# Turning the attention weighting around: context keys stationary, scaling after a trip through DRAM

## Chip, cores and metric

The kernel runs on one core of one Trainium2 chip. The metric is device time in microseconds (us) of one launch; lower is better.

## What is computed

For each of 32 batches of 128 tokens of width 128, the block adds a gated cross attention and then a gated mixture of experts:

```python
x = x + tanh(g_xattn) * attention(layernorm(x), ctx)      # 16 heads of 64; ctx: 128 keys of width 64
x = x + tanh(g_ffn)   * experts(layernorm(x))             # 32 experts, 8 picked per token of 2 of 4 groups, 1 shared
# attention: scores = (ln Wq)(ctx Wk)^T / 8; out = softmax(scores) (ctx Wv) Wo + bo
```

## The kernel before

The host only lays arrays out. Weights are folded once: Wq and Wk of a head become one 128 x 64 matrix (`a_hi`, `a_lo`), Wv and Wo one 64 x 128 matrix (`c_pair`, tanh of the gate in it). So a head is scores = (ln x A) ctx^T, u = exp(scores - max) ctx, output = (u / row sum) C. Two heads make a pair (q = 0, 1: rows 0 to 63 and 64 to 127), a batch has eight pairs, in two halves h of four pairs.

The 32 batches go in eight chunks of four (c, b; batch t = 4c + b). All synchronisation is written by hand with semaphores, and each engine runs its own list in program order: a wait holds everything behind it on that engine. The attention of one batch:

- TensorE, half 0: `max_scores` of batch t + 2 (tokens on partitions, for the row maxima), `scores` of t (keys on partitions), `transpose_max` of t + 1, `transpose_u` and two `weigh` of batch t - 1 (h = 1), `project_out` of t - 2. Half 1: `max_scores`, `scores`, `transpose_u` of t - 1, `weigh` of t (h = 0, q = 0 and 1). At odd b, `g_project` for half of the next chunk stands between those two `weigh`; at b = 1, `transpose_norm` (L1033) of the next chunk in half 0.
- `weigh` (L1097) has the probabilities as stationary matrix and the 64 context columns and a column of ones as moving one: four products of 65 columns for one (h, q). u stands with tokens on partitions, the row sum in its own column.
- VectorE: `take_max` (L706), two per half, `normalise` (L714, a reciprocal of four sums and a product that reads PSUM), `residual`, `g_low`, and the layer norm chains `ln_level` (L627): 14 levels of tiny instructions per chunk of four batches, once for the first norm (next chunk) and once for the second (previous chunk).
- ScalarE: `exp_of`, `max_out`, `ut_out` (u transposed, PSUM to SBUF), at odd b `g_high`. GpSimd splits contexts and expert weights into two halves and adds a bias. SyncE issues every DMA; `load_max_row` (L279) is the one in the loop that depends on fresh results.

Then the experts (`experts_of` on each engine): 17 units u per chunk, three engines deep; TensorE has nine products of 512 columns per unit, VectorE two, GpSimd one. Routing of chunk c + 1 (48 VectorE steps) and the second norm's application run between the units of chunk c. The routing weights go through DRAM (`store_rows`, then `load_group`, 2 x 256 KB broadcast) before `weigh_hidden` can use them. At the seam of attention and experts, the routing of chunk 0 runs beside the last attention chunk (`SEAM`).

## Time and profile before

| | |
|---|---|
| time, median of 3 runs | 703.14 us (701.32 to 707.08) |
| the profiled execution | 703.62 us, its span in the trace 701.8 us |
| TensorE busy (matmul) | 683.8 us, 97% |
| VectorE / ScalarE / GpSimd busy | 73% / 47% / 38% |
| granted TensorE clock, mean | 0.995 |

Spans are from first to last instruction; the 1.8 us between the span and its execution's time are outside every engine. Busy times come from one profiled execution. A busy TensorE only says that some matmul was in flight.

### The profile page before, as it was taken

How to read it: one execution, taken by the hardware profiler on the slowest of the kernel's cores; microseconds unless marked ns; L12 is line 12 of the kernel's file. 1: busy time of each engine (PE TensorE's matmuls, PEld its weight loads, DVE VectorE, ACT ScalarE, POOL GpSimd, SP SyncE). 2: the span in 40 equal slices, each digit the busy share in tenths (PEclk: the TensorE clock that was granted, in tenths of full speed). 3: DMA queues.
4: the chain of work that ended last, by engine and by line, in shares of the span. 5: the costliest groups of instructions: out<-in, count | busy, mean ns of one | idle time of the engine just before them, and what ended most of it. 6: DMA issues, size and time to landing. Idle time of an engine off the chain costs nothing.

```text
span 701.8 us, 15942 instructions
## 1 busy us (share of the span) xinstructions
PE 683.8 (97%) x4700; PEld 580.8 (83%) x4700; DVE 512.6 (73%) x1640; ACT 331.3 (47%) x627; POOL 266.2 (38%) x316
## 2 busy tenths in 40 slices
PE   8799999999999999999999898999999999999997
PEld 6589889888889889889998686878787888878785
DVE  6775877768767777687567596877778686969565
ACT  3243344434443344434344555555555555555553
POOL 4212121222122121212310264656666565756654
PEclk9999999999999999999999999999999999999999
DMA  5401000000000000000000554535363636455550
GB/s 134 131 19 27 17 19 18 22 18 18 18 18 18 19 17 18 24 18 18 18 2 1 115 131 95 136 90 138 86 160 79 165 91 155 106 124 136 111 148 15
DMA packets 44815, 47.27 MB, mean 67 GB/s; under 512 B 11744, under 2 KB 27232, under 8 KB 44768
## 3 DMA queue, kind: packets, MB, share of 16 engines
q1 hardware_dynamic: 44768, 46.72, 27.4%
q8 instruction: 21, 0.34, 0.2%
q14 instruction: 26, 0.21, 0.1%
HBM read 43.81 MB, written 2.62 MB: 66 GB/s over the span
## 4 chain that ended last, share of the span: by engine, by line
PE 89%; POOL 4%; issue 4%; DVE 1%; DMA 1%; ACT 0%; POOLq 0%; SPq 0%; DVEq 0%
PE bank L1105 16%; PE bank L1029 13%; PE bank L1031 13%; PE bank L1030 13%; PE bank L1137 8%; PE bank L1065 5%; PE bank L1113 5%; POOL halves L457 4%; PE bank L1085 3%; PE bank L1091 2%; PE bank L1088 2%; PE bank L1094 2%; PE bank L1152 1%; PE bank L1036 1%; PE bank L1075 1%
## 5 line engine op out<-in xcount | busy, mean ns | idle before, releaser
L457 POOL TENSOR_TENSOR halves<-area,halves 128x512 fp32r<-128x512 f32 x135 | 174.6, 1293 | 145.0 <-ACT halves L580 139.4
L537 ACT ACTIVATE area<-bank 128x512 f32<-128x512 f32 x128 | 69.5, 595 | 190.7 <-PE bank L1094 190.7
L593 ACT ACTIVATE area<-bank 128x512 f32<-128x512 f32 x136 | 81.3, 597 | 112.6 <-PE bank L1031 111.8
L989 DVE TENSOR_TENSOR bank<-area,bank 128x512 f32<-128x512 f32 x128 | 88.6, 692 | 55.4 <-PE bank L1031 54.7
L1105 PE MATMUL bank<-ctx_keys,area 128*128 128x65 f32 x1024 | 123.1, 271 | 0.0
L1105 PEld LDWEIGHTS bank<-ctx_keys,area 128*128 128x128 f32 x1024 | 120.6, 192 | 0.4 <-issue 0.4
L1029 PE MATMUL bank<-x2t_hi,w_hi 128*128 128x512 f32 x272 | 110.4, 406 | 2.2 <-DVE area L997 2.1
L1031 PE MATMUL bank<-x2t_lo,w_hi 128*128 128x512 f32 x272 | 107.0, 393 | 0.0
L710 DVE TENSOR_REDUCE row_max<-bank 128x4 f32<-128x512 f32 x128 | 82.0, 684 | 33.5 <-PE bank L1065 28.9
L1030 PE MATMUL bank<-x2t_hi,w_lo 128*128 128x512 f32 x272 | 106.5, 392 | 0.0
L405 POOL TENSOR_TENSOR ctx_hi<-ctx_raw,ones_col 128x128 fp32r<-128x128 f32 x32 | 12.8, 400 | 238.7 <-PE bank L1094 232.2
L580 ACT ACTIVATE halves<-area 128x512 fp32r<-128x512 f32 x136 | 85.0, 626 | 17.8 <-DVE area L997 12.8
L997 DVE TENSOR_TENSOR area<-bank,wbc 128x512 f32<-128x512 f32 x128 | 86.3, 679 | 3.6 <-DMA wbc<-rows_dram 3.6
L1137 PE MATMUL bank<-c_pair,area 128*128 128x128 f32 x512 | 63.8, 278 | 0.7 <-ACT area L490 0.7
L1029 PEld LDWEIGHTS bank<-x2t_hi,w_hi 128*128 128x128 f32 x272 | 51.4, 189 | 14.5 <-DVE area L997 4.3
L1031 PEld LDWEIGHTS bank<-x2t_lo,w_hi 128*128 128x128 f32 x272 | 51.3, 189 | 11.7
L723 DVE TENSOR_TENSOR area<-bank,inv_sum 128x256 f32<-128x256 f32 x128 | 54.3, 425 | 9.1
L1137 PEld LDWEIGHTS bank<-c_pair,area 128*128 128x128 f32 x512 | 59.7, 192 | 0.9 <-ACT area L490 0.9
L1030 PEld LDWEIGHTS bank<-x2t_hi,w_lo 128*128 128x128 f32 x272 | 51.6, 190 | 10.1
L1029 PE MATMUL bank<-halves,w_hi 128*128 128x512 f32 x136 | 54.3, 399 | 1.1 <-POOL halves L457 1.1
L1031 PE MATMUL bank<-halves,w_hi 128*128 128x512 f32 x136 | 53.9, 397 | 0.0
L1030 PE MATMUL bank<-halves,w_lo 128*128 128x512 f32 x136 | 53.9, 396 | 0.0
(119 smaller groups left out, 1099.0 us busy)
## 6 DMA issues: line engine op xcount, KB each, us to landing
wbc<-rows_dram SPq DMA_DIRECT2D x128, 256.0 KB, 4.4
w_raw<-experts SPq DMA_DIRECT2D x32, 102.0 KB, 2.0
ctx_raw<-ctx_t SPq DMA_DIRECT2D x64, 32.0 KB, 2.1
out<-area SPq DMA_DIRECT2D x7, 256.0 KB, 4.2
ctx_keys<-ctx_nat SPq DMA_DIRECT2D x32, 32.0 KB, 1.8
max_rows<-max_t SPq DMA_DIRECT2D x64, 4.0 KB
area<-wq_t SPq DMA_DIRECT2D x1, 512.0 KB, 4.6
area<-wo SPq DMA_DIRECT2D x1, 512.0 KB, 4.4
```

Source lines behind the costliest of these rows:

```text
L457: nc.gpsimd.tensor_tensor(hid_lo[:, u % SLOTS, :], hid[:, u % HIDS, :], raw(hid_hi[:, u % SLOTS, :]), ALU.subtract).then_inc(hidlo_ready, 1)
L537: nc.scalar.activation(probs_t[:, k, :, :], st_ps[q][:].rearrange("p (h n) -> p h n", h=4), ACT.Exp)\
L580: nc.scalar.activation(hid_hi[:, u % SLOTS, :], hid[:, u % HIDS, :], ACT.Copy).then_inc(hidhi_ready, 1)
L593: nc.scalar.activation(silu_g[:, u % 2, :], gate_ps[u % 2][:], ACT.Silu).then_inc(silu_ready, 1)
L710: nc.vector.tensor_reduce(row_max[:, parity, first:first + 4], ps[q][:].rearrange("p (h m) -> p h m", h=4), AX_X, ALU.max)\
L989: nc.vector.tensor_tensor(up_ps[u % UPS][:], silu_g[:, u % 2, :], up_ps[u % UPS][:], ALU.mult)\
L997: nc.vector.tensor_tensor(hid[:, u % HIDS, :], up_ps[u % UPS][:], wbc[:, group % WBC_SLOTS, i, :], ALU.mult).then_inc(hid_ready, 1)
L1029: nc.tensor.matmul(ps, wh, xh, start=start, stop=False)
L1030: nc.tensor.matmul(ps, wl, xh, start=False, stop=False)
L1031: return nc.tensor.matmul(ps, wh, xl, start=False, stop=stop)
L1105: ins = nc.tensor.matmul(u_ps[q][:, i * (CD + 1):(i + 1) * (CD + 1)], probs_t[:, k, i, :], ctx_keys[:, b, :], start=True, stop=True)
L1137: ins = nc.tensor.matmul(ps, u_t[:, parity, p, :], c_pair[:, p, :], start=p == 0, stop=p == PAIRS - 1)
```

## The change

- `weigh`: the context keys are the stationary matrix (65 columns: keys and ones for q = 0; 128 columns: ones, 63 zeros, keys for q = 1), the probabilities of four heads the moving one: one product of 512 columns per (h, q). u comes out transposed, with the row sums in partition 64 (q = 0) or 0 (q = 1). `transpose_u` and its evacuation `ut_out` go.
- ScalarE copies u from PSUM to SBUF (`u_out`, four per batch, 65 or 128 x 512) in place of two `ut_out`.
- Row sums: SyncE spreads each row of 1024 sums over 64 partitions (`spread_sums`, two DMAs), VectorE takes one reciprocal of 128 x 16 (`invert`), SyncE stores it to DRAM (`store_inverse`) and reads it back as a broadcast to 2 x 64 partitions (`spread_inverse`, two DMAs of 64 x 1024, one buffer). VectorE then scales u from SBUF with two instructions of 64 x 1024 (`normalise(t, ., q)`), both inputs in SBUF. The projection comes one batch later (t - 3 in place of t - 2).
- Layer norms: statistics are taken batch by batch (second norm) or all in the first chunk (first norm); the Newton chain runs over 4, 4 and 24 batches for the first norm and over 28 and 4 for the second.
- Seam: the second norm and the routing of chunk 0 start earlier, and the last batches' reciprocal, scaling, projection and residual (`LATE`, `NORM_AT`) move into the first experts' units; the last four batches' second norm moves into chunk 1. Routing of chunk 1 starts one unit earlier.
- `load_raw` is one DMA of 128 partitions, `load_keys` writes the keys twice.

```diff
-LN_STEPS = 2 * CB + 5 + 3 * NEWTON_STEPS
+RSTD_LEVELS = 3 + 3 * NEWTON_STEPS
+RSTD_STEPS = RSTD_LEVELS + 1
...
-LN_LEVELS = 5 + 3 * NEWTON_STEPS
-LN_AT = {0: range(0, 9), 1: range(9, 12), 2: range(12, LN_LEVELS)}
-LN2_AT = {4: range(0, 6), 5: range(6, 9), 6: range(9, LN_LEVELS)}
-SEAM = (1, 7, 11, 15, 18, 21)
+LN_AT = {0: range(0, 5), 1: range(5, 9), 2: range(9, RSTD_LEVELS)}
+AHEAD = 2
+STATS_AT = {3: (2,), 4: (3,), 5: (4,), 6: (5, 6), 7: (7,)}
+NB_SEAM = (NCH - 2) * CB
+SEAM = {4: (1, 7), 5: (7, 13), 6: (13, 16), 7: (16, 21)}
+LATE = {NB - 2: 5, NB - 1: 11}
+NORM_AT = {(2, 1): ((NB - 2, 0), (NB - 2, 1)), (6, 1): ((NB - 1, 0),), (7, 1): ((NB - 1, 1),)}
...
-        u_norm = area[:, 2:4, :].rearrange("p a (h q d) -> p a h q d", h=PAIRS, q=2)
+        u_even = area[:, 2:4, :].rearrange("p q (h n) -> p q h n", h=2)
...
-        ctx_keys = sb("ctx_keys", [P, CB, CD + 1])
+        ctx_keys = sb("ctx_keys", [P, CB, 3 * CD])
+        u_odd = sb("u_odd", [P, 2, 2, CT])
+        u_raw = (u_even, u_odd)
+        sums = sb("sums", [P, 2, HEADS])
+        inverse = sb("inverse", [P, 2, HEADS])
+        inverse_bc = sb("inverse_bc", [P, 2, CT])
...
+            def spread_sums(t, parity):
+                wait_first(u_ready, 4 * t + 4)
+                for q in range(2):
+                    row = CD if q == 0 else 0
+                    sp.dma_start(sums[rows(q), parity, :], u_raw[parity][row:row + 1, q, :, :]).then_inc(sums_in, 16)
+            def store_inverse(t, parity):
+                wait_first(inverse_ready, t + 1)
+                sp.dma_start(inverse_dram[parity].rearrange("q (p n) -> (q p) n", n=HEADS), inverse[:, parity, :])\
+                    .then_inc(inverse_out, 16)
+            def spread_inverse(t, parity):
+                wait_first(inverse_out, 16 * t + 16)
+                for q in range(2):
+                    wait_first(norm_ready[q], t)
+                for q in range(2):
+                    sp.dma_start(inverse_bc[rows(q), :, :].rearrange("p h n -> p (h n)"),
+                                 inverse_dram[parity, q:q + 1, :].broadcast_to([HD, 2 * CT])).then_inc(inverse_in, 16)
...
+                    if not (last and b == CB - 1):
+                        load_max_row(t + 1, (b + 1) % 2, t - 1)
+                    if not (first and b == 0):
+                        spread_sums(t - 1, (b - 1) % 2)
                     if not last:
                         wait_first(ctx_ready, t + 1)
                         load_raw(b, (t + CB) * P)
                     if not (last and b >= 2):
                         wait_first(wsplit_ready, t + 1)
                         load_weights(b % 2, (t + 2) * WSTEP)
-                    if not (last and b == CB - 1):
-                        load_max_row(t + 1, (b + 1) % 2, t - 1)
                     if not (last and b > 0):
                         wait_first(u_done, 4 * t)
                         load_keys((b - 1) % CB, t - 1 + CB)
+                    if not (first and b == 0):
+                        store_inverse(t - 1, (b - 1) % 2)
+                        spread_inverse(t - 1, (b - 1) % 2)
...
+            spread_sums(NB - 1, (NB - 1) % 2)
             store_rows(0)
             for g in range(WBC_SLOTS):
                 load_group(0, g)
+            store_inverse(NB - 1, (NB - 1) % 2)
+            spread_inverse(NB - 1, (NB - 1) % 2)
...
-            def ut_out(t, parity, r):
-                act.wait_ge(ut_done, 2 * t + r + 1)
-                wait(act, attn_done, t - 1)
-                nc.scalar.activation(u_t[:, parity, 4 * r:4 * r + 4, :],
-                                     ut_ps[:].rearrange("p (h n) -> p h n", h=4), ACT.Copy).then_inc(ut_ready, 1)
+            def u_out(t, parity, h, q):
+                act.wait_ge(u_done, 4 * t + 2 * h + q + 1)
+                wait(act, norm_ready[q], t - 1)
+                held = slice(0, CD + 1 if q == 0 else P)
+                nc.scalar.activation(u_raw[parity][held, q, h, :], u_ps[q][held, :], ACT.Copy).then_inc(u_ready, 1)
...
+            def batch_stats(t, b):
+                wait_first(x2_ready, t + 1)
+                nc.vector.bn_stats(bn6[:, 1, b, :], tile_of(t)).then_inc(ln_step[1], 1)
+            def batch_mean(t, b):
+                wait_first(ln_step[1], 2 * t + 1)
+                nc.vector.bn_aggr(mean_var_now[:, b, :], bn6[:, 1, b, :]).then_inc(ln_step[1], 1)
...
+            def rstd_level(which, n, batches, level):
+                width = batches.stop - batches.start
+                scratch = ln_small if width <= 2 * CB else ln_large
...
-            def normalise(t, parity, h, q):
-                k = 2 * h + q
-                u = u_ps[q][:, 0:4 * (CD + 1)].rearrange("p (h d) -> p h d", h=4)
-                dve.wait_ge(u_done, 4 * t + k + 1)
-                wait(dve, inv_ready, 4 * t + k - 3)
-                nc.vector.reciprocal(inv_sum[:, k, :], u[:, :, CD]).then_inc(inv_ready, 1)
-                dve.wait_ge(inv_ready, 4 * t + k + 1)
-                wait(dve, ut_done, 2 * (t - 2) + h + 1)
-                nc.vector.tensor_tensor(u_norm[:, parity, pairs_of(h), q, :], u[:, :, 0:CD],
-                                        inv_sum[:, k, :].unsqueeze(2).broadcast_to([P, 4, CD]), ALU.mult)\
-                    .then_inc(norm_ready, 1)
+            def invert(t, parity):
+                dve.wait_ge(sums_in, 32 * t + 32)
+                wait(dve, inverse_out, 16 * (t - 1))
+                nc.vector.reciprocal(inverse[:, parity, :], sums[:, parity, :]).then_inc(inverse_ready, 1)
+            def normalise(t, parity, q):
+                dve.wait_ge(inverse_in, 32 * t + 32)
+                wait(dve, attn_done, t - 1)
+                nc.vector.tensor_tensor(u_t[rows(q), parity, :, :].rearrange("p i n -> p (i n)"),
+                                        u_raw[parity][rows(q), q, :, :].rearrange("p h n -> p (h n)"),
+                                        inverse_bc[rows(q), :, :].rearrange("p h n -> p (h n)"), ALU.mult)\
+                    .then_inc(norm_ready[q], 1)
...
-                            residual(t - 2)
-                        if not last:
+                        if h == 0:
+                            if not first:
+                                batch_stats(t - CB, b)
+                        else:
+                            if not (first and b == 0):
+                                invert(t - 1, (b - 1) % 2)
+                            if not (first and b < 2):
+                                normalise(t - 2, b % 2, 1)
+                            if not (first and b < 3):
+                                residual(t - 3)
+                            if not first:
+                                batch_mean(t - CB, b)
+                                if b == CB - 1:
+                                    keep_means(t - b - CB)
+                        if first:
+                            if step_of_chunk == 0:
+                                chunk_stats(1)
                             for level in LN_AT.get(step_of_chunk, ()):
-                                ln_level(0, c + 1, t - b + CB, level)
+                                rstd_level(0, 1, slice(CB, 2 * CB), level)
                             if step_of_chunk == 2:
-                                ln_apply(c + 1, t - b + CB)
-                        if not first:
-                            for level in LN2_AT.get(step_of_chunk, ()):
-                                ln_level(1, c - 1, t - b - CB, level)
+                                ln_apply(1, CB)
+                        elif not last and step_of_chunk == 1:
+                            ln_apply(c + 1, t - b + CB)
                         if last:
-                            if step_of_chunk == 1:
+                            if step_of_chunk == 0:
+                                for level in range(RSTD_LEVELS):
+                                    rstd_level(1, 0, slice(0, NB_SEAM), level)
                                 ln2_apply(0, 0)
-                            if step_of_chunk == 6:
-                                route_chunk_0(SEAM[0], SEAM[1])
-                            if step_of_chunk == 7:
-                                route_chunk_0(SEAM[1], SEAM[2])
-                        for q in range(2):
-                            if h == 1:
-                                if q == 1 and b % 2 == 1 and not last:
-                                    g_low(2 * c + 2 + b // 2, b // 2)
-                                normalise(t, b % 2, 0, q)
-                            elif not (first and b == 0):
-                                normalise(t - 1, (b - 1) % 2, 1, q)
+                            if step_of_chunk == 4:
+                                ln2_apply(1, CB)
+                            if step_of_chunk in SEAM:
+                                route_chunk_0(*SEAM[step_of_chunk])
+                        if h == 0 and not (first and b < 2):
+                            normalise(t - 2, b % 2, 0)
+                        if h == 1 and b % 2 == 1 and not last:
+                            g_low(2 * c + 2 + b // 2, b // 2)
...
-            for q in range(2):
-                normalise(NB - 1, (NB - 1) % 2, 1, q)
-            route_chunk_0(SEAM[3], SEAM[4])
-            residual(NB - 2)
-            route_chunk_0(SEAM[4], SEAM[5])
-            ln2_apply(1, CB)
-            residual(NB - 1, u_ps[0][:, 0:D])
+            residual(NB - 3)
...
+                if first and (u, place) == (0, 1):
+                    invert(NB - 1, (NB - 1) % 2)
+                if first:
+                    for t, q in NORM_AT.get((u, place), ()):
+                        normalise(t, t % 2, q)
+                if first and place == 1:
+                    for t, at in LATE.items():
+                        if u == at:
+                            residual(t, misc_ps[:, 0:D])
+                if c == 1 and place == 1:
+                    if u == 1:
+                        for b in range(CB):
+                            batch_stats(NB - CB + b, b)
+                    if u == 2:
+                        for b in range(CB):
+                            batch_mean(NB - CB + b, b)
+                        keep_means(NB - CB)
+                    if 3 <= u < 3 + RSTD_LEVELS:
+                        rstd_level(1, 1, slice(NB_SEAM, NB), u - 3)
...
-                wait(pe, norm_ready, 4 * t + k - 1)
+                wait(pe, u_ready, 4 * t + k - 1)
                 if k == 0:
                     pe.wait_ge(keys_in[b], 16 * loads)
-                for i in range(4):
-                    ins = nc.tensor.matmul(u_ps[q][:, i * (CD + 1):(i + 1) * (CD + 1)],
-                                           probs_t[:, k, i, :], ctx_keys[:, b, :], start=True, stop=True)
-                ins.then_inc(u_done, 1)
-            def transpose_u(t, parity, r):
-                pe.wait_ge(norm_ready, 4 * t + 2 * r + 2)
-                wait(pe, ut_ready, 2 * t + r)
-                for i in range(4):
-                    ins = nc.tensor.transpose(ut_ps[:, i * P:(i + 1) * P],
-                                              u_norm[:, parity, 4 * r + i, :, :].rearrange("p q d -> p (q d)"), ident[:])
-                ins.then_inc(ut_done, 1)
+                keys = ctx_keys[:, b, 0:CD + 1] if q == 0 else ctx_keys[:, b, CD:3 * CD]
+                nc.tensor.matmul(u_ps[q][0:CD + 1 if q == 0 else P, :], keys,
...
-                        transpose_u(t - 1, (b - 1) % 2, 0)
                         for q in range(2):
-                            weigh(t - 1, (b - 1) % CB, 1, q, c + 1)
-                    if b == 1:
-                        pe.wait_ge(ut_ready, 2 * t - 1)
+                            weigh(t - 1, (b - 1) % CB, 1, q, c + (b > 0))
+                    if b == (0 if last else 1):
                         transpose_norm(c + 1, ut_ps)
-                    if last and b == 2:
-                        route(0, scores_ps[1])
+                    if last and b == 1:
+                        route(0, ut_ps)
                     if last and b == CB - 1:
-                        pe.wait_ge(x2_ready, t - 2)
-                    if not (first and b < 2):
-                        project_out(t - 2, b % 2, t + 1 if last and b == CB - 1 else t + 2)
+                        pe.wait_ge(max_ready, 4 * NB)
+                        transpose_norm(c + 2, scores_ps[1])
+                    if last and b == CB - 1:
+                        pe.wait_ge(x2_ready, t - 3)
+                    if not (first and b < 3):
+                        project_out(t - 3, (b + 1) % 2, t + 1 if last and b == CB - 1 else t + 2)
...
-            transpose_u(NB - 1, (NB - 1) % 2, 0)
             for q in range(2):
                 weigh(NB - 1, CB - 1, 1, q, NCH)
+            transpose_weights(0, y_ps)
             pe.wait_ge(exp_ready, 4 * NB)
-            pe.wait_ge(x2_ready, NB - 2)
-            project_out(NB - 2, NB % 2, NB)
-            transpose_u(NB - 1, (NB - 1) % 2, 1)
-            project_out(NB - 1, (NB - 1) % 2, NB, u_ps[0][:, 0:D])
+            pe.wait_ge(x2_ready, NB - 3)
+            project_out(NB - 3, (NB - 3) % 2, NB)
...
-                        transpose_weights(0, y_ps)
-                        pe.wait_ge(x2_ready, NB - 1)
-                        transpose_norm(NCH + 1, misc_ps)
+                        pe.wait_ge(x2t_ready, 2)
+                    for t, at in LATE.items():
+                        if first and u == at - 1:
+                            pe.wait_ge(x2_ready, t)
+                            project_out(t, t % 2, NB, misc_ps[:, 0:D])
```

## Rows read from the trace of the kernel before

**Rows 1.** The page, busy times of the whole span.
```profile
PE 683.8 (97%) x4700; PEld 580.8 (83%) x4700; DVE 512.6 (73%) x1640; ACT 331.3 (47%) x627; POOL 266.2 (38%) x316
```

**Rows 2.** Stretches: us; busy (instructions) of PE, PEld, DVE, ACT, POOL; clock, DMA share, GB/s.
```profile
157.40:202.80 45.40, 45.34 (x411) 40.71 (x410) 33.98 (x109) 18.50 (x39) 9.67 (x20) 1.00 0.07 19
...
399.00:404.00 5.00, 4.48 (x13) 3.59 (x14) 4.13 (x14) 3.33 (x7) 2.69 (x3) 0.68 1.06 225
```

**Rows 3.** Chain that ended last, 340 to 410 us: start, us, what.
```profile
347.03 1.84 PE bank L1137 x16
348.87 0.59 PE bank L1065 x8
...
350.45 0.59 PE bank L1113 x4
351.04 1.74 PE bank L1105 x16
...
354.55 0.44 PE bank L1113 x4
```

**Rows 4.** Timeline, weight loads, 22 to 25 us: start, us, engine, line.
```profile
22.96 0.19 PEld L1152 LDWEIGHTS bank<-c_pair 128*128 128x128 f32 x1 [0.24 <-issue]
23.39 0.19 PEld L1152 LDWEIGHTS bank<-c_pair 128*128 128x128 f32 x1 [0.24 <-issue]
```

**Rows 5.** Instruction groups by form, VectorE: count, busy, mean ns, idle before.
```profile
L710 DVE TENSOR_REDUCE row_max<-bank 128x4 f32<-128x512 f32 x128 | 82.0, 684 | 33.5 <-PE bank L1065 28.9 <-PE bank L1075 3.6 <-issue 0.9
L723 DVE TENSOR_TENSOR area<-bank,inv_sum 128x256 f32<-128x256 f32 x128 | 54.3, 425 | 9.1
L701 DVE TENSOR_TENSOR halves<-bank,halves 128x512 fp32r<-128x512 f32 x64 | 43.3, 691 | 13.0 <-ACT halves L478 12.1
L720 DVE RECIPROCAL inv_sum<-bank 128x4 f32<-128x4 f32 x128 | 23.0, 180 | 32.3 <-PE bank L1105 29.7
```

**Rows 6.** Timeline of a batch with odd b, 202 to 208 us.
```profile
203.89 2.68 ACT L478 ACTIVATE halves<-bank 128x512 fp32r<-128x512 f32 x4 [0.62 <-PE bank L1031]
...
204.52 2.77 DVE L701 TENSOR_TENSOR halves<-bank,halves 128x512 fp32r<-128x512 f32 x4 [0.65 <-ACT halves L478]
...
207.42 0.19 PEld L1085 LDWEIGHTS bank<-halves,ctx_hi 64*128 64x128 f32 x2 [0.20 <-issue]
```

**Rows 7.** Chain that ended last, routing weights through DRAM.
```profile
391.26 0.60 ACT weight_rows L571
391.94 1.67 DMA rows_dram<-weight_rows
...
394.41 4.27 DMA wbc<-rows_dram
398.78 0.70 DVE area L997
```

**Rows 8.** DMA issues: KB each, median us to landing; issue time of one (ns min/median/max).
```profile
ctx_keys<-ctx_nat SPq DMA_DIRECT2D x32, 32.0 KB, 1.8
...
area<-wq_t SPq DMA_DIRECT2D x1, 512.0 KB, 4.6
...
L284 SPq DMA_DIRECT2D max_rows<-max_t x64: 624/690/1192, 21.5 to 366.1; - x64
```

**Rows 9.** Timeline, VectorE and GpSimd together, at 211, 215 and 694 us.
```profile
211.80 0.16 DVE L673 SCALAR_TENSOR_TENSOR guess<-newton,guess 128x4 f32<-128x4 f32 x1
...
215.01 0.46 POOL L408 TENSOR_TENSOR ctx_lo<-ctx_raw,ctx_hi 128x128 fp32r<-128x128 f32 x1
...
215.06 0.43 DVE L673 SCALAR_TENSOR_TENSOR guess<-newton,guess 128x4 f32<-128x4 f32 x1
...
694.42 1.28 POOL L457 TENSOR_TENSOR halves<-area,halves 128x512 fp32r<-128x512 f32 x1 [0.30 <-ACT halves L580]
...
694.97 1.27 DVE L1018 TENSOR_TENSOR halves<-area,halves 128x512 fp32r<-128x512 f32 x1 [0.70 <-ACT halves L580]
```

**Rows 10.** Waits, 384 to 430 us: total, times, longest us.
```profile
PE bank L1129 <- DVE weight L863: 2.2, 1, 2.2
PE bank L1029 <- DVE area L997: 2.1, 1, 2.1
```

238 lines of the change are left out of this document (116 added, 122 removed).

## The prediction

> **What bounds the kernel now.** I read the page first: a matmul is in flight 97% of the span and VectorE is next with 73% [rows 1]. Then the stretches: a whole attention chunk takes 45.4 us and TensorE stands still for 0.06 us of it [rows 2], so the loop over chunks 1 to 6 is TensorE's work and little else. The chain that ended last says what this work is: in a batch the u products (L1105, 16 records of 4 heads by 65 columns by two) take 1.74 us per half, the two groups of transposes of u (L1113) 0.59 and 0.44 us, the projection 1.84 us [rows 3]. One thing besides TensorE is nearly late already: at odd b, g_high ends at 206.57 and g_low at 207.29, and the scores start at 207.42 after a wait of 0.2 us [rows 6]. So the path has two candidates: TensorE's list, and VectorE's list where it ends in g_low.
>
> **TensorE's part.** A product of 512 fp32 columns is two records, and their weight loads follow each other by 0.43 us [rows 4]. So the new weighing costs 8 x 0.43 = 3.44 us a batch, against 2 x 1.74 = 3.48: nothing is won there. The transposes go: 1.03 us a batch. A pair of batches (even b, odd b) takes (45.4 - 0.44) / 2 = 22.5 us now, the 0.44 being the transposes of the norm at b = 1; TensorE alone would need 22.5 - 2.1 = 20.4. If g_low stays as late as its input allows, it holds the next scores some 0.5 us, so 20.9. That is the floor: a chunk of 42.3 us, 3.1 less.
>
> **VectorE's part.** Removed per batch: four reciprocals (0.18) and four products (0.425) [rows 5], 2.4 us, and about 2 us of tiny norm steps. Added: one reciprocal (0.2, estimate from the same row), two products of 64 x 1024, one bn_stats and one bn_aggr as before. The price of a product: 256 elements take 425 ns and 512 take 691 ns [rows 5], so 1.04 ns an element and 1.22 us for 1024 (estimate). But those rows read one input from PSUM, and the new instruction reads both from SBUF. The only long row of that kind, L1018, takes 1.27 us for 512 elements; GpSimd was in an instruction until 695.70, though, and L1018 started at 694.97 and ended at 696.24 [rows 9]. A Newton step of the same kind takes 0.16 us alone and 0.43 when a GpSimd instruction that started before it ends at 215.47 [rows 9]. So I read L1018 as 0.73 us held plus 0.54 of its own, and take 1.22 us for 1024, with 2.4 us (double L1018's) as the other end. The wait costs about 0.3 us where GpSimd's five instructions of a batch run; those start after the second scores of a batch, where the second product stands. VectorE's work is then about 8 us of a batch's 10.5: it isn't the bound by volume.
>
> The Trainium skill (SBUF — State Buffer, section "SBUF: two separate sides") has the rule for this: VectorE with two SBUF inputs and GpSimd take one shared port pair by an exclusive lock, and the loser waits for the whole instruction. The rows agree (0.43 against 0.16). It speaks against the change, as 64 long instructions of that kind come in; by VectorE: DVE Perf Modes, section "The TRN2 errata", a free one of 1024 would take (1024 + 151) / 0.96 = 1.22 us, an estimate of that page.
>
> **The new chain, which I think sets the loop.** VectorE's list is in order, and for a batch t it is: take_max (2), normalise(t - 2, 0); take_max (2), invert(t - 1), normalise(t - 2, 1), residual, mean, g_low. Both invert and normalise wait for DMAs, and behind a waiting normalise(., 0) stand the maxima that TensorE needs for g_project and the next max_scores, and then g_low. Its data leaves in the half before. The way from the end of a producer through a store to DRAM and a broadcast of two times 256 KB back is in the trace: weight_rows ends at 391.86, the store takes 1.67, the second load's 4.27 ends at 398.68, VectorE starts at 398.78: 6.9 us [rows 7]. There ten more loads follow directly, here none; a single transfer of the same 512 KB lands in 4.6 us from its issue where this pair needs 5.0 [rows 8]. I take 6.6, with 5.5 and 7.5 as ends. Now the loop of one pair, started at invert in the even batch:
>
> - invert 0.2, round trip 6.6, normalise(., 0) 1.22, two take_max 1.28 (82.0 / 64), invert 0.2, normalise(., 1) 1.22 + 0.3, residual and mean 0.5, g_low 2.77, handover to the scores 0.13 [rows 5, 6, 7]: 14.4 us.
> - From there TensorE: scores 0.99, transpose of the maxima 0.12, weighing 1.72, projection 1.84, max_scores 0.59, then 0.2 and two take_max 1.28 until VectorE reaches invert [rows 3, 5]: 6.7 us. The sums come on a second way: scores and weighing 2.8, u_out 0.8, SyncE's two issues (0.69 each, as load_max_row's, which now stands before them) and a landing of 1.8 (the small key load) [rows 8]: 6.4 to 7.1, the latter if a landing from one partition is slower. I take 6.9.
>
> Sum 21.3 us a pair against 22.5 now. At b = 1 xt_low (0.69) also stands behind normalise(., 0). A chunk: 2 x 21.3 + 0.7 = 43.3, against 45.4. So of the 4.1 us that TensorE's list gets shorter, half goes into the wait for the round trip; six chunks give 12.6 us. Even batches don't stall on it: there a whole g_project (2.9 us) lies in the interval.
>
> **What hides the other edits.** The new DMA issues: SyncE gets about 3 us more a batch, of 10.5, and waits some 2 us in store_inverse and spread_inverse; load_max_row behind them is due only when maxima are evacuated, about 1 us later. If the round trip grew by more than 2 us, this would be late too and hit the scores. ScalarE: four copies of 0.6 for two, of 10.5 us; it is 47% busy [rows 1]. GpSimd can be held by 1.22 us, it idles two thirds of the attention.
>
> First chunk: statistics of 24 batches and the long Newton chain put some 12 us more on VectorE beside 28 us of its usual work; I give it no gain (3 either way). Last chunk: the transposes and two waits go, but the second norm of chunk 0 (a chain of 28 batches, some 2.6 us, then ln2_apply) now has to be ready 3 us after the chunk begins and TensorE waits for it about 3 us; no gain, 2 either way. The two late projections only change place.
>
> Start of the experts: TensorE stood 2.1 us for the first routing weights [rows 10], and its granted clock was 0.68 of full in the 5 us that followed, a mean of the 2.4 and the 1.2 GHz level, which costs 1.6 us [rows 2]. With routing done earlier both go: 3.7 us. The wait of 2.2 us for chunk 1's weights [rows 10] goes too, as the norm chain leaves chunk 0; but four products of 1.22 (each held by GpSimd for a part of its 1.28) come into chunk 0 and the chain into chunk 1, so I count 1.0.
>
> Sum: 12.6 + 3.7 + 1.0 = 17.3 us. Span 701.8 - 17.3 = 684.5, and with the 1.8 outside 686.3. The profiled execution (703.6) is half a microsecond above the median of 703.1, so 686.
>
> **Rivals.** *TensorE's floor* (round trip at 5.5 us or less, or more slack in g_project than I give): 3.1 x 6 = 18.6 us, and 3 from the first chunk, with the 4.7: 677. For it: only 19 GB/s of other traffic in a chunk [rows 2]. Against: it needs 1.4 us less than a complete chain in this trace took. *A slower round trip* (8 us in all, or sums that land after 3.5 us: one source partition of 4 KB in pieces of 64 B, of which no row shows the landing): 1.1 us more a pair, the chunk is at 45.5, only the seam gains: 699. *VectorE at half rate*, the one on the other side: if two fp32 SBUF inputs really cost 1.27 us per 512, each normalise is 2.4 us, and both stand in the loop: 23.7 us a pair, a chunk of 48.1, 2.7 x 6 = 16 us lost, some 6 more in first and last chunk and units: 721. It decides from 1.8 us per normalise on, where the pair is at 22.5. For it L1018's plain duration; against it the overlap above.
>
> **Chances.** Forecast 0.48 (678 to 696), TensorE's floor 0.22, slower round trip 0.18, half rate 0.12. A measurement here tells 1% from no change. Faster by over 1% (below 696): 0.46 + 0.22 = 0.68; within 1%: 0.19; slower: 0.13. The range leaves out half rate and the tail of the floor: 671 to 706.
>
> **What would show it.** Chunk period near 43.3 with TensorE idle about 1 to 2 us at g_project or the scores behind it, once per pair; VectorE waits for inverse_bc at odd b only; normalise near 1.22 us and more where GpSimd works; spread landing near 4.3; no wait for the first routing weights. I am wrong if TensorE has no idle time in the chunks (floor), if normalise is 2 us and over, or if invert waits for the sums in every batch.

## The result and the profile after

The changed kernel takes 695.6 us (median of 4 runs, 694.6 to 696.8) where the kernel before took 702.5 in the same session: a ratio of 0.989, 95% interval 0.985 to 0.993. Run again on another chip beside the kernel before it gave 693.6 us and 0.986 (0.982 to 0.990). So it is about 1.2% faster. The forecast was 686 us, 17.3 less than the profiled execution before; the profiled execution after takes 695.3 us with a span of 693.5, which is 8.3 less.

The page of the changed kernel, busy times, beside [rows 1]:

```profile
PE 662.6 (96%) x3676; PEld 477.5 (69%) x3676; DVE 504.2 (73%) x1329; ACT 369.2 (53%) x691; POOL 285.8 (41%) x317
```

TensorE lost 21 us of busy time, but the span only 8. To see where the rest went, I cut both spans at the same three events: the start of g_low of b = 3 in chunk 0, the same in chunk 6, and the first expert matmul. The rows are stretches, with the columns of [rows 2]. Before:

```profile
0.00:68.30 68.30, 61.70 (x470) 49.97 (x471) 44.42 (x124) 25.17 (x49) 18.85 (x44) 0.98 0.31 78
68.30:340.60 272.30, 271.94 (x2451) 244.23 (x2451) 203.94 (x655) 110.79 (x224) 58.40 (x122) 1.00 0.07 19
340.60:389.20 48.60, 47.15 (x412) 42.34 (x410) 33.45 (x142) 21.36 (x39) 5.80 (x10) 1.00 0.03 7
389.20:701.80 312.60, 303.03 (x1374) 244.26 (x1373) 230.79 (x720) 173.98 (x317) 183.12 (x142) 0.99 0.49 117
```

After:

```profile
0.00:66.30 66.30, 58.37 (x349) 37.51 (x350) 47.64 (x142) 29.91 (x56) 20.05 (x45) 0.95 0.40 100
66.30:330.80 264.50, 255.11 (x1695) 168.34 (x1695) 185.14 (x345) 140.05 (x272) 73.11 (x118) 0.99 0.29 71
330.80:376.70 45.90, 41.06 (x239) 24.29 (x239) 33.38 (x116) 26.16 (x49) 7.98 (x13) 1.00 0.26 66
376.70:693.50 316.80, 308.09 (x1399) 247.33 (x1397) 238.05 (x727) 173.07 (x316) 184.71 (x142) 0.99 0.49 117
```

First chunk -2.0, six chunks -7.8, last chunk -2.7, experts +4.2: together -8.3. The forecast was 0, -12.6 and, over the last two stages, -4.7, where they gave +1.5. The cuts don't hold the same work in each stretch: the projection comes one batch later and the last two come late, so two projections (of about 1.95 us and 16 records each, L1137 before and L1210 after) stand in the first stretch before and one after, six and five in the last chunk, none and two in the experts. In the six chunks TensorE was busy for 99.9% before and stands still for 9.4 us after. What it waited for in them (total, times, longest us):

```profile
PE bank L1146 <- DVE halves L753: 3.6, 5, 0.9
PE bank L1166 <- DVE halves L753: 3.0, 11, 0.3
PE bank L1110 <- DVE row_max L762: 1.7, 6, 0.4
```

So 6.6 of the 9.4 us are waits for g_low (L753), of max_scores (L1146) and scores (L1166), and most of the rest are waits for the maxima (L762), of g_project (L1110). Three single chunks:

```profile
155.40:199.62 44.22, 42.39 (x283) 27.83 (x282) 30.59 (x55) 23.37 (x47) 12.79 (x22) 1.00 0.28 71
199.62:244.13 44.51, 43.00 (x280) 28.02 (x279) 29.93 (x55) 23.05 (x45) 11.88 (x20) 0.96 0.28 71
244.13:287.12 42.99, 41.76 (x282) 27.65 (x281) 30.05 (x56) 23.15 (x46) 12.17 (x21) 1.00 0.28 73
```

The chunks are unequal, where before the same five periods took 45.34 to 45.37 us each. The granted clock is a part of it: 0.96 in the second row, where a stretch at half clock lies, and 1.00 in the others.

The new instructions, groups by form on VectorE, beside [rows 5]:

```profile
L776 DVE TENSOR_TENSOR area<-u_odd,inverse_bc 64x1024 f32<-64x1024 f32 x32 | 41.1, 1283 | 45.1 <-DMA inverse_bc<-inverse_dram 44.6
...
L776 DVE TENSOR_TENSOR area<-area,inverse_bc 64x1024 f32<-64x1024 f32 x32 | 40.1, 1254 | 9.6 <-DMA inverse_bc<-inverse_dram 9.0
```

The first group, the odd batches' u, does most of the waiting. One such wait on the timeline (start, us, engine or SyncE's queue, line), from invert in an even batch to g_low in the odd one, beside [rows 6, 7]:

```profile
232.04 0.25 DVE L770 RECIPROCAL inverse<-sums 128x16 f32<-128x16 f32 x1
...
232.22 0.39 SPq L274 DMA_DIRECT2D ctx_keys<-ctx_nat  x1
...
232.72 0.40 SPq L301 DMA_DIRECT2D inverse_dram<-inverse  x1
...
234.70 1.12 SPq L310 DMA_DIRECT2D inverse_bc<-inverse_dram  x2
...
239.32 1.22 DVE L776 TENSOR_TENSOR area<-u_odd,inverse_bc 64x1024 f32<-64x1024 f32 x1 [3.70 <-DMA inverse_bc<-inverse_dram]
...
240.47 1.27 DVE L762 TENSOR_REDUCE row_max<-bank 128x4 f32<-128x512 f32 x2
...
241.19 0.19 PEld L1110 LDWEIGHTS bank<-xnt_hi,a_hi 128*128 128x128 f32 x1 [0.72 <-DVE row_max L762]
...
244.13 2.47 DVE L753 TENSOR_TENSOR halves<-bank,halves 128x512 fp32r<-128x512 f32 x4
```

The round trip takes 7.03 us from the end of invert (232.29) to the start of the product that needs it (239.32). The maxima stand behind this product on VectorE, and TensorE waits 0.72 us for them before g_project. The store is issued only after load_keys, 0.43 us behind the end of invert.

At the start of the experts, the chain of work and then the timeline:

```profile
385.04 2.21 DVE area L776
387.24 0.34 issue
387.58 3.44 PE bank L1210 x16
```

```profile
383.80 3.44 DVE L776 TENSOR_TENSOR area<-area,inverse_bc 64x1024 f32<-64x1024 f32 x2
...
384.63 1.53 POOL L494 TENSOR_TENSOR halves<-area,halves 128x512 fp32r<-128x512 f32 x1 [0.79 <-ACT halves L620]
```

Two products of 1.22 us each take 3.44 us together: the second starts at 385.04 and takes 2.21, while a GpSimd instruction runs from 384.63 to 386.16. TensorE waits 1.99 us for them, and the projection (L1210) then takes 3.44 us where the next one, at 405.66, takes 1.95. The stretch says why: its granted clock is 0.55.

```profile
387.60:391.10 3.50, 3.50 (x17) 3.50 (x18) 3.47 (x7) 1.27 (x3) 1.27 (x1) 0.55 0.36 72
```

The Trainium skill (SBUF — State Buffer, section "SBUF: two separate sides") has VectorE, with two SBUF inputs, and GpSimd share a port pair by a lock, the loser waiting for the whole instruction. The rows above agree: the two products take 1.0 us more than twice 1.22.

### The profile page after: what moved, and what is told of

Its sections match the earlier page's. It is cut to its first block and busy times, and to the rows that moved or that the text cites. A ratio compares the mean times of both kernels' runs of the same rounds, so it can differ in the third digit from the quotient of the medians.

```text
span 693.5 us, 13643 instructions
## 1 busy us (share of the span) xinstructions
PE 662.6 (96%) x3676; PEld 477.5 (69%) x3676; DVE 504.2 (73%) x1329; ACT 369.2 (53%) x691; POOL 285.8 (41%) x317
## 5 line engine op out<-in xcount | busy, mean ns | idle before, releaser
L1186 PE MATMUL bank<-area,ctx_keys 128*65 128x512 f32 (+1 forms) x256 | 127.4, 611 | 0.8 <-ACT u_odd L528 0.8
L1110 PE MATMUL bank<-x2t_hi,w_hi 128*128 128x512 f32 x272 | 110.8, 407 | 1.6 <-DVE area L1078 1.6
L762 DVE TENSOR_REDUCE row_max<-bank 128x4 f32<-128x512 f32 x128 | 81.9, 682 | 35.0 <-PE bank L1146 32.5
L440 POOL TENSOR_TENSOR ctx_hi<-ctx_raw,ones_col 128x128 fp32r<-128x128 f32 x32 | 18.0, 562 | 216.4 <-DMA ctx_raw<-ctx_t 216.4
L1078 DVE TENSOR_TENSOR area<-bank,wbc 128x512 f32<-128x512 f32 x128 | 86.5, 681 | 0.4 <-DMA wbc<-rows_dram 0.4
L776 DVE TENSOR_TENSOR area<-u_odd,inverse_bc 64x1024 f32<-64x1024 f32 x32 | 41.1, 1283 | 45.1 <-DMA inverse_bc<-inverse_dram 44.6
L1210 PEld LDWEIGHTS bank<-c_pair,area 128*128 128x128 f32 x512 | 62.8, 196 | 14.4 <-issue 11.7
L1210 PE MATMUL bank<-c_pair,area 128*128 128x128 f32 x512 | 64.1, 280 | 3.1 <-DVE area L776 2.0
L1186 PEld LDWEIGHTS bank<-area,ctx_keys 128*65 128x65 f32 (+1 forms) x256 | 38.0, 166 | 41.8 <-issue 40.2
L1110 PEld LDWEIGHTS bank<-x2t_hi,w_hi 128*128 128x128 f32 x272 | 51.3, 189 | 14.7 <-DVE area L1078 4.5
L1146 PEld LDWEIGHTS bank<-ctx_hi,halves 64*128 64x128 f32 x512 | 33.5, 186 | 36.7 <-issue 29.8
L1110 PE MATMUL bank<-halves,w_hi 128*128 128x512 f32 x136 | 54.3, 399 | 1.1 <-POOL halves L494 1.1
```

Source lines behind the costliest of these rows:

```text
L762: nc.vector.tensor_reduce(row_max[:, parity, first:first + 4], ps[q][:].rearrange("p (h m) -> p h m", h=4), AX_X, ALU.max)\
L1078: nc.vector.tensor_tensor(hid[:, u % HIDS, :], up_ps[u % UPS][:], wbc[:, group % WBC_SLOTS, i, :], ALU.mult).then_inc(hid_ready, 1)
L1110: nc.tensor.matmul(ps, wh, xh, start=start, stop=False)
L1186: nc.tensor.matmul(u_ps[q][0:CD + 1 if q == 0 else P, :], keys, probs_t[:, k, :, :].rearrange("p i n -> p (i n)"), start=True, stop=True). ...
L1210: ins = nc.tensor.matmul(ps, u_t[:, parity, p, :], c_pair[:, p, :], start=p == 0, stop=p == PAIRS - 1)
```

## Experiments

There are four theories. A: the loop over the chunks is set by the way from invert through the round trip to g_low. B: it is set by TensorE's list. C: it is set by the volume of VectorE's work. Seam theory: the experts lost their gain to VectorE's long products. "Chunk" below is the mean over the five periods between g_low of b = 3 in chunks 1 and 6 of the profiled execution; "experts" is from the first expert matmul to the end. All ratios are to the kernel before on the same chip. The runs lie on different chips, so times of two of them are compared closely only where it says so. The diffs are shortened; "..." marks what is left out.

**short_round_trip**

```diff
+                    store_inverse(...)          # ahead of load_keys
                     load_keys((b - 1) % CB, t - 1 + CB)
-                    store_inverse(...)
                     spread_inverse(...)
...
-                dve.wait_ge(inverse_in, 32 * t + 32)
+                dve.wait_ge(inverse_in[q], 16 * t + 16)   # spread q raises its own
```

> Two edits that only shorten the round trip: store_inverse is issued ahead of load_keys (saves its issue, 0.39 us, in even batches), and each half of u waits for its own load of inverse_bc (saves the second issue, 0.54 us, for the first half). Theory A: 0.9 us less on the chain of each pair, of which 0.7 to 0.9 reach TensorE until its floor of 20.9 us a pair; with some 14 pairs 8 to 12 us, 684 to 688 us. Theory B: no change, 694 to 697 us. Theory C: no change.

The result is 678.7 us, a ratio of 0.962 (0.958 to 0.965), and a chunk of 41.4. No stretch at half clock lies between the start-up and the last microseconds. This is far more than B or C allow, and more than A forecast. The stretch of the six chunks, and the same wait as above (invert at 178.70):

```profile
65.10:313.90 248.80, 247.84 (x1680) 166.51 (x1680) 185.28 (x347) 138.60 (x271) 69.15 (x117) 1.00 0.30 76
```

```profile
178.70 0.25 DVE L771 RECIPROCAL inverse<-sums 128x16 f32<-128x16 f32 x1
...
184.38 1.22 DVE L777 TENSOR_TENSOR area<-u_odd,inverse_bc 64x1024 f32<-64x1024 f32 x1 [1.99 <-DMA inverse_bc<-inverse_dram]
...
186.18 1.29 DVE L763 TENSOR_REDUCE row_max<-bank 128x4 f32<-128x512 f32 x2 [0.58 <-PE bank L1147]
```

VectorE still waits for the loads, but behind that it waits for TensorE (0.58 us): the order is turned round, and TensorE stands still for 1.0 us in 248.8.

**normalise_later**

```diff
+                            if b % 2 == 1 and not (first and b < 2):   # h == 1, after invert
+                                normalise(t - 2, b % 2, 0)
...
-                        if h == 0 and not (first and b < 2):
+                        if h == 0 and b % 2 == 0 and not (first and b < 2):
                             normalise(t - 2, b % 2, 0)
```

> In odd batches normalise(., 0) moves from the first half of the batch to the second, next to normalise(., 1), so that no maximum stands behind the wait for the loads. Theory A: the wait of about 4 us on inverse_bc is gone, but the half up to g_low is now full on VectorE (1.28 + 0.24 + 2.44 + 0.5 us ahead of g_low, with 0.3 to 0.7 held by GpSimd), so g_low comes 0.5 to 1 us after its input and holds the scores: chunk 42.5 to 44, 685 to 696 us. Theory B: g_low later and nothing won: 700 us. Theory C: as A.

The result is 690.2 us, 0.978 (0.974 to 0.982), with a chunk of 43.2, in A's range but no shorter than the changed kernel's 43.3 (changed_again below). What the run won lies in the first chunk (62.9 us in place of 66.0) and the period behind it (43.8 in place of 45.1). VectorE's waits for inverse_bc fall from 53.6 to 4.4 us in the whole run, and TensorE's for g_low, at max_scores and scores, rise to 9.2 us in place of 6.6. So the wait can be removed without shortening the round trip, but the delay comes back through g_low.

**late_project**

```diff
-LATE = {NB - 2: 5, NB - 1: 11}
+LATE = {NB - 2: 7, NB - 1: 11}
```

> The late projection of batch 30 moves from unit 4 to unit 6 of chunk 0's experts, two units behind its normalise. Theory A (seam): the wait of TensorE for normalise (1.99 us) and the half clock over the projection behind it (1.7 us) both go: 3.7 us, 692 us. Rival: both products are long in VectorE's way in any case, gate products behind them are late, TensorE waits the same 2 us at the next unit: 695 to 696 us.

The result is 692.2 us, 0.981 (0.977 to 0.985), but the experts take 316.8 us as before the edit: the wait for normalise is gone, and a new one for weigh_hidden (L1078) has come at a later product of the experts, again with half clock over what follows:

```profile
384.00 0.79 PE L1110 MATMUL bank<-x2t_hi,w_hi 128*128 128x512 f32 x1 [2.67 <-DVE area L1078]
```

The rival held. What made the profiled execution shorter is the loop (chunk 42.9 in place of 43.8), which this edit doesn't touch: that is the spread of the changed kernel itself.

**changed_again**, the changed kernel as it is:

> The changed kernel itself, unedited, so that the three others have it beside them on the same chip. Theory A: the chunk is set by a chain through three DMA landings, so its length moves with them: periods between 42.8 and 44.5 us, 690 to 697 us. The theory that the loop is TensorE's list would want equal periods to a tenth, as the kernel before had.

The result is 693.6 us, 0.986 (0.982 to 0.990), with periods of 43.24, 42.94, 43.37, 43.38 and 43.60, mean 43.3. It ran on the same chip as the next three.

**constant_factor**

```diff
-                dve.wait_ge(inverse_in, 32 * t + 32)
...
-                                        inverse_bc[rows(q), :, :]...
+                                        c_pair[rows(q), :, :]...
```

> normalise multiplies by the tile c_pair in place of inverse_bc and doesn't wait for the loads; all DMAs are still issued (left out: the division by the right sums). Theory A: short_round_trip was already at TensorE's own length (41.4 us a chunk in all six periods), so this one has the same 41.4 and 677 to 680 us. Rival (the round trip still costs something there, as VectorE waited 20.8 us for inverse_bc): a period of 40 to 41 us, 668 to 675 us.

This kernel leaves out the division by the right sums. (A tile of its own for the constant doesn't fit in SBUF beside wbc, so c_pair, of the same size, stands in.) The result is 677.6 us, 0.961 (0.958 to 0.965), and a chunk of 41.4. That is TensorE's own length, and short_round_trip had reached it; the 20.8 us that VectorE still waited for inverse_bc there cost nothing. All DMAs are still issued here, so neither SyncE's queue nor the traffic held the loop: VectorE's wait for the landing did.

**store_first** and **own_load**, the two edits of short_round_trip, each alone:

> Only the order of SyncE's issues: store_inverse ahead of load_keys. Theory A, one us for one us: 0.39 us less a pair, 0.8 a chunk, 5 to 6 us in all: 5 below the changed kernel of this call. Theory A2 (the chain's delay comes back more than once, as u_out, the weighing and the half clock follow it): 8 to 12 us below. Theory B (this order costs nothing): as the changed kernel.

> Only the waits: each half of u waits for its own load of inverse_bc. Theory A, one us for one us: 0.54 us less a pair, 1.1 a chunk, 7 to 8 us below the changed kernel of this call. Theory A2: 9 to 14 below. Theory B: as the changed kernel. If store_first and own_load together give more than the two of them at once did (17), each alone already reaches TensorE's floor.

The results are 685.4 us, 0.973 (0.970 to 0.976), chunk 41.8, and 679.8 us, 0.965 (0.962 to 0.969), chunk 41.4. These are 8.2 and 13.8 us below changed_again, more than the one for one that A expected. I measured the piece itself, from the start of invert in an even batch to the start of normalise(., 0) in the odd one, a mean of 12 (13 for short_round_trip): 7.38 us in changed_again, 6.74 in store_first, 6.40 in own_load, 5.69 with both. The edits shorten it by 0.64 and 0.98 us, not by the 0.39 and 0.54 of an issue. Where store_first's extra comes from is seen in its trace:

```profile
182.86 0.25 DVE L771 RECIPROCAL inverse<-sums 128x16 f32<-128x16 f32 x1
...
183.21 0.33 SPq L301 DMA_DIRECT2D inverse_dram<-inverse  x1
...
183.88 0.39 SPq L274 DMA_DIRECT2D ctx_keys<-ctx_nat  x1
...
184.87 1.12 SPq L310 DMA_DIRECT2D inverse_bc<-inverse_dram  x2
```

From the store's issue to the issue of the broadcast, which waits for the store, it is 1.66 us here and 1.98 (232.72 to 234.70) where the store stands behind load_keys; the means over the loop are 1.71 and 1.98. So the store also lands sooner. Against the piece, the loop's gain is 0.74 us a pair for 0.64, nearly one for one. For own_load it is 0.96 a pair for 0.98, and there the chunk is at TensorE's floor of 41.4.

**two_stores**, the same test in the other direction:

```diff
-                sp.dma_start(inverse_dram[parity]...)
+                for target in (second_dram, inverse_dram):
+                    sp.dma_start(target[parity]...)
```

> The changed kernel with a second store of the reciprocals, to a DRAM tensor that nobody reads, ahead of the real one: one more issue of 0.33 to 0.4 us in each round trip. Theory A one for one: 0.4 us more a pair, 0.8 a chunk: 44.1 us; in all 5 to 6 us more, 699. Theory A2 (as the edits that shortened it gave 0.65 for an issue of 0.39): 0.65 to 0.75 a pair, 44.6 to 44.8 us, 702 to 704.

The result is 698.3 us, 0.990 (0.987 to 0.994); the piece takes 7.71 us (+0.33), the chunk 44.2 (+0.9, 0.45 a pair). The real store is issued 0.53 us later than in changed_again, and the issue that waits for it comes 0.21 us sooner behind it (1.77 in place of 1.98), as the store is no longer the one directly behind load_keys. The chunk came out as A forecast (44.1) and under the 44.6 to 44.8 of an amplification in the loop, so store_first's surplus was the store that lands sooner. Theory A stands.

**seam_spread**

```diff
-NORM_AT = {(2, 1): ((NB - 2, 0), (NB - 2, 1)), (6, 1): ((NB - 1, 0),), (7, 1): ((NB - 1, 1),)}
+NORM_AT = {(1, 1): ((NB - 2, 0),), (2, 1): ((NB - 2, 1),), (6, 1): ((NB - 1, 0),), (9, 1): ((NB - 1, 1),)}
```

and LATE as in late_project.

> The changed kernel with the late products of the last two batches spread out: normalise(30, 0) into VectorE's idle gap in unit 1, normalise(31, 1) from unit 7 to unit 9, and batch 30's projection from unit 4 to unit 6. Theory A (the seam lost its gain to VectorE's long products standing together ahead of the gate and weigh products): the waits of 2.0 us on normalise, of 1.6 us on weigh_hidden and the half clock behind them go, from the first expert matmul to the end 312 to 313.5 us in place of 316.8, whole kernel 689 to 690. Rival (as in late_project, the wait only moves on to the next unit): 316 to 317 us there, 692 to 694 in all.

The result is 692.5 us, 0.984 (0.980 to 0.988), with experts of 315.7. One wait for weigh_hidden is 0.54 us, another 2.06 at 397 us, with half clock behind it. This was mostly a miss: 312 to 313.5 had been expected, and order alone buys 1 us there.

**norm_transposes_later**

```diff
-                    if b == (0 if last else 1):
+                    if b == 1 and not last:
                         transpose_norm(c + 1, ut_ps)
...
+                    if last and b == 0:          # after the last weigh; x2t_out likewise
+                        transpose_norm(c + 1, ut_ps)
```

> The changed kernel with the transposes of chunk 0's second norm at the end of the last chunk's batch 0 in place of its middle, and x2t_out with them, so that the Newton chain of 24 batches is hidden. Theory A: TensorE's wait of 1.9 to 2.4 us for xn goes and nothing waits for what follows: 2 us less, 691.5 us. Rival (the last chunk is bound by VectorE's list, the routing and the round trips, so the wait only turns up later in it): 693 to 694 us.

The result is 689.0 us, 0.979 (0.975 to 0.983); the last chunk takes 43.6 us in place of 46.0 in changed_again. The wait for xn was real and nothing took its place.

**all_edits**: the four together.

> short_round_trip's two edits, seam_spread's and norm_transposes_later's together. Theory A: their gains add, as they lie in different stages: 678.7 - 4 - 2 = 672 to 674 us. Rival: 677 to 679 us, as short_round_trip.

The result is 675.1 us, 0.959 (0.955 to 0.963), with a last chunk of 43.5, experts of 314.1 and a chunk of 41.4. That lies between the theory (672 to 674) and the rival (677 to 679). Against short_round_trip the medians differ by 3.6 us and the profiled spans by 3.0, of which 2.4 lie in the last chunk and 1.0 in the experts.

**tiny_late_products**

```diff
+                if isinstance(t, int) and t >= NB - 2:
+                    nc.vector.tensor_tensor(u_t[rows(q), parity, 0, 0:16], ...)   # 16 columns, not 1024
+                    return
```

> The changed kernel, with the four products of batches 30 and 31 inside the experts cut from 64x1024 to 64x16 elements (left out: the rest of these products, so that the last two batches' projections read old values). Theory A (VectorE's long products are what the seam lost): the waits of 2.0 and 1.6 us and the half clock (1.5) go, from the first expert matmul to the end 311.5 to 312.5 us in place of 316.7. Rival (the projections and the routing inside chunk 0 cost it, whoever divides): 315 to 317.

This kernel leaves out most of the late products. The result is 688.6 us, 0.977 (0.971 to 0.983); the experts:

```profile
374.40:687.20 312.80, 306.04 (x1399) 245.91 (x1397) 231.88 (x727) 172.89 (x316) 183.48 (x142) 1.00 0.49 118
```

The experts take 4.0 us less than in the changed kernel (316.8, and 316.7 in changed_again), all of it in their first chunk: four products of 1.22 us cost TensorE 4 us. So the larger part of what the experts lost is shown to be these products; one wait of 1.4 us for weigh_hidden stays without them.

**Placement.** Every later expert chunk takes longer than before: with TensorE hardly idle and the same matmuls, 37.75 us before (4 in 151.0) and 38.0 after (5 in 190.0). I moved the tiles in SBUF by unused gaps. The allocator rounds each tile up to 32 bytes, which the expectations of pad_16 and pad_64 don't reckon with, so that they name wrong places; the real ones, modulo 128 bytes, are in the table. The relative theory says that weights and moving data at the same place modulo 128 are fast; the absolute theory says that some places are fast and others slow.

```diff
+        gap_0 = sb("gap_0", [P, 8])     # pad_16: 4, pad_64: 3 floats ahead of a_hi, and 8 ahead of row_max
         area = sb("area", [P, 6, 1024])
```

> The changed kernel with an unused tile of 16 bytes a partition ahead of a_hi, which brings w_hi, w_lo, x2t_hi, x2t_lo and halves to the addresses modulo 64 that they had in the kernel before. Theory A (their placement slows the matmuls of the experts): expert chunks of 37.76 us, 1.6 us less. Rival (something else, as the instruction stream): 37.96, as the changed kernel.

> The same with 12 bytes ahead of a_hi and 32 ahead of row_max: halves, w_hi, w_lo, x2t_hi and x2t_lo all begin at a multiple of 64 bytes. Theory A: expert chunks of 37.76 us or less. Rival: 37.96.

> The changed kernel with unused gaps that put every large tile at 32 modulo 128 bytes. Relative theory (weights and moving data at the same place modulo 128 are read without a loss): expert chunks of 37.49 us, as pad_64, 3.5 us less than the changed kernel in all. Absolute theory (96 is the good place, 32 the bad one): 37.96 us or more.

> The changed kernel with every large tile that TensorE reads at 0 modulo 128 bytes. Relative theory: expert chunks of 37.49 us, 690 us in all. Absolute theory: as all_32 or worse.

> The kernel before, with every large tile that TensorE reads at 0 modulo 128 bytes. Relative theory: expert chunks of 37.49 in place of 37.76 us, 2 us less in the experts and some tenths in each attention chunk of 45.36: 699 to 701 us. Absolute theory: as the kernel before or slower.

| kernel | halves | w_hi, x2t_hi | an expert chunk, us | kernel, us | ratio |
|---|---|---|---|---|---|
| before | 64 | 96 | 37.75 | | |
| changed | 64 | 32 | 38.0 | 693.6 (again) | 0.986 |
| pad_16 | 96 | 64 | 37.96 | 690.6 | 0.981 |
| pad_64 | 96 | 96 | 37.48 | 689.1 | 0.977 |
| all_32 | 32 | 32 | 37.52 | 688.5 | 0.976 |
| all_0 | 0 | 0 | 37.48 | 685.3 | 0.973 |
| before_all_0 | 0 | 0 | 37.8 | 703.8 | 1.000 |

The stretches behind the column, from one transpose of y to another, for the changed kernel and all_0 (5 chunks each):

```profile
434.50:624.50 190.00, 189.75 (x867) 152.81 (x866) 148.22 (x487) 109.67 (x201) 116.05 (x90) 1.00 0.50 121
```

```profile
427.10:614.50 187.40, 186.57 (x866) 152.66 (x865) 147.81 (x487) 109.57 (x201) 115.94 (x90) 1.00 0.48 122
```

before_all_0, 2 chunks:

```profile
555.30:630.90 75.60, 75.49 (x347) 61.04 (x346) 58.11 (x191) 43.67 (x81) 46.41 (x36) 1.00 0.47 121
```

In the changed kernel the three gaps under which a chunk takes 37.5 us (0.5 less) are those with w_hi and halves at the same place, which speaks for the relative theory and against the absolute one. In the kernel before the same places as all_0's give nothing. So the placement moves an expert chunk by up to 1.4%, but neither theory is the rule, and it isn't shown that the places are why the changed kernel's chunk is 0.25 us longer than the one before: at the same places the changed kernel's is 0.3 us shorter. 37.96 and 38.0 are the same time; the other differences of pad_16's run lie elsewhere.

**everything_0**: all_edits with all_0's gaps.

> all_edits with all_0's gaps. Relative theory: 675 less 3.5 to 4: 671 us. Absolute theory: 675 us.

The result is 671.1 us, 0.951 (0.948 to 0.955), the best version: 4.9% faster than the kernel before. Its last two stages:

```profile
315.00:358.50 43.50, 41.81 (x249) 25.57 (x248) 32.94 (x115) 27.04 (x50) 9.86 (x13) 1.00 0.26 71
358.50:669.10 310.60, 302.32 (x1399) 245.48 (x1397) 235.74 (x727) 173.16 (x316) 184.12 (x142) 1.00 0.47 119
```

## Why the prediction was right and wrong

The prediction had the sign right, but only half of the gain came. Of the 9.0 us by which the span missed the forecast, 6.2 lie at the expert start and in the routing, and this is the step that failed; 4.8 lie in the six chunks, whose mechanism was right, and 2.0 came back in the last chunk.

- **TensorE's part**: right. Weighing gives nothing and the transposes go: constant_factor's chunk of 41.4 is within 0.2 us of 45.4 less four times 1.03.
- **Price of a product, 1.22 us**: right (medians 1220 and 1222 ns); the half-rate rival is out.
- **The new chain**: right in kind, as short_round_trip, constant_factor and two_stores show, and close in size. VectorE waits for inverse_bc mostly in odd batches, and TensorE stands still for g_low and the maxima, for 0.8 us a pair where 1 to 2 were forecast. The round trip was taken at 6.6 us from the end of invert and measured 7.1 (7.38 less the 0.25 of invert); that the pair still came out as forecast, 43.3 us a chunk in changed_again, is in part luck, as the rest of the pair was taken too long by about as much. I also treated 43.3 as a fixed number. It hangs on DMA landings, and in six kernels with the same loop and placement it was 42.9 to 43.8; the profiled execution after was the longest of them. Its five later periods won 7.8 us where 10.5 were forecast.
- **TensorE's floor, 42.3**: too long by 0.9. I let g_low hold the scores by 0.5 us a pair there as well; when the round trip is short, it doesn't. So the change had 4 us a chunk to give, not 3.1, and gave 1.6 to 2.
- **First chunk, 0**: right. Its stretch is 2.0 us shorter, but by one projection of 1.95 that left it. The period behind it, counted as one of the six, takes 45.5 us and won nothing of its 2.1. In it VectorE runs 77 instructions, against 55 to 57 in the later ones (the norm chain of 24 batches); with short_round_trip the same period is 41.9, so there too it is mostly the round trip. What adds the rest isn't shown.
- **Last chunk, 0**: inside its margin of 2. Its stretch is 2.7 us shorter. One projection of 1.95 went out and two groups of transposes of 0.60 came in, which leaves 2.0 won. The wait for xn was 1.9, forecast 3; norm_transposes_later took it away.
- **Expert start and routing, 4.7**: this step failed. The two waits of [rows 10] and the half clock behind the one for the first routing weights did go, worth 5.9 us. But of the four products I wrote "so I count 1.0", from their own length and for TensorE's gate only, without following who waits for VectorE there: the projection (2.0), weigh_hidden (1.6), and a new stretch at half clock on the first (1.5). That is 5.1 us, and tiny_late_products gave back 4.0 of it. (In changed_again the waits there were 1.9 and 3.1 us without half clock, and the stage was as long.) The later expert chunks add 1.6 (8 times 0.2), which nothing in the trace before could tell, and whose cause stays open. The sum: 312.6 + 2.7 moved - 5.9 + 5.1 + 1.6 = 316.1, of 316.8 measured.
- **The clock**: I took a half-clock stretch away and put none in. The trace after has four between start-up and end, at 53, 64, 204 and 388 us, and the trace before two, at 36 and 401. The one at 204 cost some 1.8 us (0.04 of the 44.51 us of its chunk), and it came behind two waits for g_low, of 0.93 and 0.32 us. So a wait that I priced at its own length can cost another 1.5 to 1.8 us. Which of them will is not settled: in changed_again the same wait of 1.88 us at the seam had none behind it.

Together, with the moved work taken out: 0 stayed 0, 12.6 became 7.8, 0 became 2.0, and 4.7 became -1.5.

## What to carry to other kernels

When a step goes through DMAs on an in-order engine, ask what stands behind its wait, and shorten the way before moving it: two edits of issue order and of semaphores, for which no work was saved, brought 2.4% here (0.986 to 0.962), more than the whole change. Work moved out of a loop into "slack" has to be followed through every engine that waits for the one that does it; spreading it bought only 1 us where the receiving engine was busy for 78% already (148.22 of 190.00 us). Compare a stage in which nothing was changed as well: that is how the effect of placement showed.

## What the runs showed of the hardware

- Where tiles lie in SBUF changes stretches of fp32r matmuls of 512 columns by up to 1.4%: 37.48 to 38.0 us for an expert chunk of the same instructions, with TensorE idle for at most 0.8 us in five chunks. The rule stays open.
- Of two loads of 256 KB, issued 0.54 us apart, the first was worth waiting for by itself: its consumer started 0.98 us sooner (own_load) than one that waits for both.
- The store of 8 KB, issued behind the load of the keys on the same queue, took 0.3 us longer to the issue that waits for it (1.98 us against 1.71).
- A stretch at half clock came behind waits as short as 0.93 and 0.32 us, and in another execution none came behind a wait of 1.88 us. short_round_trip and everything_0 have none between start-up and end.
- The kernel before took 701.3 us at a mean granted clock of 0.997 and 707 to 709 at 0.988 to 0.990, in the same sessions. So its times from one execution to the next differ with the clock: 0.8% of 703 is 5.6 us.
